# The result of a GNN and expert layer leaves in indirect scatters from GpSimd instead of plain stores from SP

## The reference

```python
def reference(x, adj, ...):
    # _L0_gnn_ref
    h = jnp.einsum('bnd,ed->bne', x, fc_in_w) + fc_in_b
    def euler_step(h, _):
        ax = jnp.einsum('nm,bmd->bnd', adj_mx, h)
        f = alph * 0.5 * (ax - h) + h @ w_eff - h + x0
        return (h + dt * f, None)
    h, _ = jax.lax.scan(euler_step, h, None, length=N_STEPS)
    # _moe
    for e in range(E):
        h = jax.nn.gelu(tokens @ w1[e] + b1[e], approximate=False)
        y = h @ w2[e] + b2[e]
        out = out + combine[:, e:e + 1] * y
    ...
    x = x + _L0_gnn_ref(_layernorm(x, axis=-1), adj, ...)
    x = x + _L0_ffn_ref(_layernorm(x, axis=-1), ...)
    return x
```

## Time and profile before

| | us |
|---|---|
| median of 2 runs | 624.26 (621.85 to 626.67) |
| span of the profiled execution | 619.0 |
| PE busy | 566.9 |
| DVE busy | 473.5 |
| ACT busy | 290.9 |
| POOL busy | 250.2 |
| DMA queue q1 (all DMAs that SP issues), share of 16 engines | 20.9% |

### The profile page before, as it was taken

One profiled execution on the slowest core, in us unless ns is written; L12 is line 12 of the kernel. 1 busy time (PEld: TensorE's weight loads), 2 busy tenths in 40 slices (PEclk: granted clock), 3 DMA queues, 4 the chain that ended last, 5 costly groups with the idle time before them and its releaser, 6 DMA issues.

```text
span 619.0 us, 9553 instructions
## 1 busy us (share of the span) xinstructions
PE 566.9 (92%) x3023; PEld 481.9 (78%) x3023; DVE 473.5 (76%) x1090; ACT 290.9 (47%) x477; POOL 250.2 (40%) x155
## 2 busy tenths in 40 slices
PE   3999999998999799998999799998999799998796
PEld 2778988976898588976898588976898588976574
DVE  5799776779676976779676976779676985579666
ACT  4322131367415662367415662367415672257574
POOL 2230320447213751447313761447313761147355
PEclk9999999999999999999999999999999989998899
DMA  5100010360105200250105300360105200350141
GB/s 181 35 0 1 0 35 1 107 202 1 34 2 210 95 17 17 104 203 0 34 2 197 107 17 17 104 203 0 34 2 191 80 17 19 104 171 0 43 164 35
DMA packets 25759, 43.15 MB, mean 70 GB/s; under 512 B 1462, under 2 KB 20236, under 8 KB 23820
## 3 DMA queue, kind: packets, MB, share of 16 engines
q1 hardware_dynamic: 25740, 42.91, 20.9%
HBM read 38.45 MB, written 4.46 MB: 69 GB/s over the span
## 4 chain that ended last, share of the span: by engine, by line
PE 63%; DVE 20%; issue 9%; ACT 3%; POOL 2%; DMA 1%; DVEq 0%; POOLq 0%; SPq 0%; ACTq 0%
PE bank L954 19%; PE bank L956 18%; PE bank L955 18%; DVE work L818 6%; DVE scr L579 3%; DVE bn L561 2%; PE bank L1080 2%; DVE scs L557 2%; POOL scs L348 2%; DVE x L579 2%; ACT work L494 2%; DVE mv L567 1%; PE bank L973 1%; PE bank L1094 1%; DMA work<-in_adj_dram 1%
## 5 line engine op out<-in xcount | busy, mean ns | idle before, releaser
L348 POOL TENSOR_TENSOR scs<-work,scs 128x512 fp32r<-128x512 f32 x96 | 153.1, 1617 | 103.5 <-ACT scs L397 103.3
L397 ACT ACTIVATE scs<-work 128x512 fp32r<-128x512 f32 (+1 forms) x129 | 82.8, 642 | 53.6 <-DVE work L818 52.3
L494 ACT ACTIVATE work<-bank,cols 128x512 f32<-128x512 f32 x128 | 86.8, 679 | 27.3 <-PE bank L956 27.0
L818 DVE TENSOR_TENSOR work<-work,GT 128x512 f32<-128x512 f32 x90 | 87.9, 990 | 9.6 <-ACT work L494 8.9
L337 POOL TENSOR_TENSOR rstd<-ve,nhalf 128x8 f32<-128x8 f32 x16 | 29.7, 1856 | 113.6 <-DVE ve L575 113.6
L954 PE MATMUL bank<-M,GT 128*128 128x384 f32 x192 | 65.6, 342 | 0.1
L955 PE MATMUL bank<-M,GT 128*128 128x384 f32 x192 | 65.0, 339 | 0.0
L956 PE MATMUL bank<-M,GT 128*128 128x384 f32 x192 | 65.0, 338 | 0.0
L557 DVE TENSOR_TENSOR GT<-bank,GT 128x512 fp32r<-128x512 f32 x48 | 32.2, 687 | 38.3 <-ACT GT L397 38.3
L954 PE MATMUL bank<-scs,w2s 128*128 128x512 f32 x128 | 56.3, 440 | 4.4 <-DVE scs L557 2.7
L397 ACT ACTIVATE GT<-bank 128x512 fp32r<-128x512 f32 x48 | 27.7, 594 | 67.5 <-PE bank L956 63.3
(11 more groups left out here) (188 smaller groups left out, 1382.1 us busy)
## 6 DMA issues: line engine op xcount, KB each, us to landing
GT<-comb_rows SPq DMA_DIRECT2D x8, 1536.0 KB, 6.8
Q<-comb_rows SPq DMA_DIRECT2D x16, 512.0 KB, 5.8
GT<-comb_rows SPq DMA_DIRECT2D x7, 1024.0 KB, 6.2
xn<-in_x_dram SPq DMA_DIRECT2D x16, 256.0 KB, 7.6
out_dram<-outs SPq DMA_DIRECT2D x16, 256.0 KB, 2.2
GT<-comb_rows SPq DMA_DIRECT2D x7, 512.0 KB, 4.3
work<-in_adj_dram SPq DMA_DIRECT2D x4, 256.0 KB, 5.4
Q<-in_L_ffn_w_dram SPq DMA_DIRECT2D x2, 512.0 KB, 5.9
```

Of the source, the lines that this page charges most:

```text
L348: nc.gpsimd.tensor_tensor(scs[:, i % RING, 1, :], scaled[:, i % 3, :], scs[:, i % RING, 0, :].bitcast(FP32), ALU.subtract).then_inc(sc_lo_ ...
L397: return nc.scalar.activation(dst, src, ACT.Copy)
L494: nc.scalar.activation(hid[:, i % 2, :], bank[UP_BANK[i % 3]][:, :], ACT.Gelu, bias=cols[:, B1_COL + e:B1_COL + e + 1]).then_inc(gelu_done, 1)
L818: v.tensor_tensor(scaled[:, i % 3, :], hid[:, i % 2, :], bank[REP_BANK[i % 2]][:, :] if by_pe else rep(i), ALU.mult).then_inc(sc_ready, 1)
```

## The change

The two plain stores per group leave SP. In their place POOL issues, for each batch, four indirect scatters; each takes 128 partitions of `outs[:, b, t, :]` and writes them to 128 rows of the output, whose row numbers stand in a column of an integer tile `out_row`. POOL makes `out_row` once with an iota and adds 1024 (`GB * N`) to all of it for each group in `next_rows`, after it has waited for all scatters issued before. `add_out` on DVE now waits for `row_ready`, which `next_rows` counts up, instead of `out_stored`. On POOL `store(g - 1)` stands at the end of iteration g, `next_rows(g - 1)` after the first `inverse_root`, and iteration 1 is written out ahead of the loop. SP only waits at its end for all scatters (16 x 8 x 8 = 1024).

```diff
--- before.py
+++ after.py
@@ -86,6 +86,8 @@
         rank_i = sb("rank_i", [P, T, E], I32)
         rank = sb("rank", [P, T, E])
         nhalf = sb("nhalf", [P, T])
+        out_row = sb("out_row", [P, GB, NT], I32)
+        out_step = sb("out_step", [P, GB, NT], I32)
 
 
         xn = sb("xn", [P, NT, GB, D])
@@ -192,6 +194,7 @@
 
         out_add = sem("out_add")
         out_stored = sem("out_stored")
+        row_ready, store_go = sem("row_ready"), sem("store_go")
         LN_OWN = T + 2
         RT_OWN = 23
 
@@ -244,7 +247,6 @@
         @block.sync
         def _(sp):
             sp.sem_inc(out_add, 1)
-            sp.sem_inc(out_stored, 1)
             sp.dma_start(alpha_rows[:, :], alpha.rearrange("(t p) -> t p", p=P)).then_inc(alpha_in, 16)
 
             def load_x(g):
@@ -255,11 +257,6 @@
                 sp.wait_ge(x0_ready, g)
                 sp.wait_ge(xg_copied, g)
                 load_x(g)
-
-            def store(h):
-                for b in range(GB):
-                    sp.wait_ge(out_add, 1 + GB * h + b + 1)
-                    sp.dma_start(of_group(out_v, h, b), outs[:, b, :, :]).then_inc(out_stored, 16)
 
             load_x(0)
             for t in range(NT):
@@ -311,13 +308,10 @@
             with sp.Fori(1, GROUPS - 2) as g:
                 expert_weights(g - 1, g)
                 next_x(g + 2)
-                store(g - 1)
             for g in range(GROUPS - 2, GROUPS):
                 expert_weights(g - 1, g)
-                store(g - 1)
             expert_weights(GROUPS - 1)
-            store(GROUPS - 1)
-            sp.wait_ge(out_stored, 1 + 32 * GROUPS)
+            sp.wait_ge(out_stored, 16 * T * GROUPS)
 
 
         @block.gpsimd
@@ -329,7 +323,9 @@
             nc.gpsimd.iota(rank_i[:, :, :], pattern=[[0, T], [-1, E]], base=E, channel_multiplier=0)
             nc.gpsimd.memset(b2_raw, 0.0).then_inc(b2_zero, 1)
             nc.gpsimd.memset(nhalf[:, :], -0.5).then_inc(pool_own, 1)
-            pool.wait_ge(pool_own, 2)
+            nc.gpsimd.iota(out_row[:, :, :], pattern=[[N, GB], [P, NT]], base=-GB * N, channel_multiplier=1)
+            nc.gpsimd.memset(out_step[:, :, :], GB * N).then_inc(pool_own, 1)
+            pool.wait_ge(pool_own, 3)
             nc.gpsimd.tensor_copy(rank[:, :, :], rank_i[:, :, :]).then_inc(pool_const, 1)
 
             def inverse_root(n, g):
@@ -347,6 +343,26 @@
                 pool.wait_ge(sc_hi, ITEMS * h + i + 1)
                 nc.gpsimd.tensor_tensor(scs[:, i % RING, 1, :], scaled[:, i % 3, :],
                                         scs[:, i % RING, 0, :].bitcast(FP32), ALU.subtract).then_inc(sc_lo_pool, 1)
+
+            def store(h):
+
+                for b in range(GB):
+                    pool.wait_ge(out_add, 1 + GB * h + b + 1)
+                    if b == 0:
+                        pool.wait_ge(row_ready, h + 1)
+                    pool.sem_inc(store_go, 1)
+                    for t in range(NT):
+                        nc.gpsimd.indirect_dma_start(
+                            out=out.rearrange("b n c -> (b n) c"),
+                            out_offset=bass.IndirectOffsetOnAxis(ap=out_row[:, b, t:t + 1], axis=0),
+                            in_=outs[:, b, t, :], in_offset=None).then_inc(out_stored, 16)
+
+            def next_rows(h):
+
+                if not (isinstance(h, int) and h == 0):
+                    pool.wait_ge(out_stored, 16 * T * h)
+                nc.gpsimd.tensor_tensor(out_row[:, :, :], out_row[:, :, :], out_step[:, :, :],
+                                        ALU.add).then_inc(row_ready, 1)
 
             def residual(h):
 
@@ -367,6 +383,8 @@
                     residual(g - 1)
                 if not final:
                     inverse_root(0, g + 1)
+                if not first:
+                    next_rows(g - 1)
                 pool.wait_ge(xg_copied, g + 1)
                 pool.wait_ge(q_ready, T * g + T)
                 nc.gpsimd.tensor_tensor(Q[:, 0], Q[:, 0], xg[:, :, :, :], ALU.add).then_inc(xq_ready, 1)
@@ -380,15 +398,19 @@
                             item_low(g - 1, i)
                         if i == 2:
                             inverse_root(1, g)
+                    store(g - 1)
 
             iteration(0, first=True)
-            with pool.Fori(1, GROUPS - 1) as g:
+            iteration(1)
+            with pool.Fori(2, GROUPS - 1) as g:
                 iteration(g)
             iteration(GROUPS - 1, final=True)
             residual(GROUPS - 1)
             for i in range(ITEMS):
                 if i not in LOW_DVE:
                     item_low(GROUPS - 1, i)
+            next_rows(GROUPS - 1)
+            store(GROUPS - 1)
 
 
         @block.scalar
@@ -802,7 +824,7 @@
             def add_out(h, b):
                 dve.wait_ge(ot_mm, GB * h + b + 1)
                 dve.wait_ge(res_ready, h + 1)
-                dve.wait_ge(out_stored, 1 + 32 * h)
+                dve.wait_ge(row_ready, h + 1)
                 v.tensor_tensor(outs[:, b, :, :], bank[OT_BANK[b]][:, :].rearrange("p (t c) -> p t c", c=D),
                                 res[:, :, b, :], ALU.add).then_inc(out_add, 1)
```

## The result

The changed kernel took 640.24 us (median of 2 runs, 640.18 to 640.30) against 624.26 us (2 runs, 621.85 to 626.67): ratio 1.0286, interval 1.0226 to 1.0346. Run again later, six executions against 18 of the kernel before, it took 634.79 us (633.03 to 643.51) against 622.9 us: ratio 1.0176, interval 1.0134 to 1.0218. So the change costs about 1.8% in the larger set of runs, whose interval reaches over the 2%, and nearly 3% in the first pair. Each series of runs can hold a single run that is over 1.5% above the fastest of its kernel at a lower granted clock, as 643.51 and 632.85 here; the medians and ranges hold such runs, the ratios and intervals leave them out.

A forecast was written before the change was run, and what follows sets the result against it. The chain that ended last was put on PE for 63% and DVE for 20%. Loop 0, last group's experts 0 and end 6.95 gave 7.0 us, added to 624.26 for 631.2 us; range 625.5 to 646.

The forecast's parts named there:

- the case: Whole kernel: time within 2% of the kernel before, counted as no change; chance 0.69.
- c: Time for which one scatter holds POOL, chosen as 1.2 us between bounds of 0.39 and 2.41 us.
- rivals 1 and 3: First: scatter over 1.6 us, loop pays, 658.6 us, chance 0.22. Second: cheap addresses, under 0.65, 624.3 us, chance 0.08.
- The loop costs nothing: Six loop turns: four scatters fit between the adds, residual ends 1.2 us before DVE wants it; cost 0.
- Rival 2: Loop: DVE's work holds up POOL's address writing, 1.9 us per scatter there, 1.2 at the end; 646.7 us, chance 0.08.
- Last group's experts: 0 at c = 1.2, bound 1.22: Start of last group's experts: residual and item 0 end at 592.58, just in time; beyond 1.22, each 0.1 costs up to 0.4.
- DVE's scaling of item 3 (592.67) waits for that `item_low`: Last group's experts: this scaling reuses the buffer of item 0's `item_low`, so POOL's work must end by 592.67.
- The end: 8c - 2.65 = 6.95: Program end: nothing covers the last eight scatters, run from 613.8 with 2.55 us behind them; cost 6.95 us.
- the last needs 2.2 us to land and 0.35 us remain as before: Program end: after the last scatter, landing and the unchanged remainder take 2.55 us until the span ends.
- Median 5.3 us over the profiled span: Whole run: the median of the runs shown, 624.26 us, is 5.3 us above the profiled span of 619.0.
- the cases for "slower by over 2%": Whole kernel: nearly all of rival 1's 0.22, the lock-out and a little of rival 4; chance 0.30 together.
- rival 4: Order no longer fits for another reason, such as a first scatter costing several us once; 625 to 645 us, chance 0.07.

The follow-up runs named there:

- The four extra scatters: Changed kernel plus four more scatters to an unread tensor behind the second add of groups 0 to 6 (92 in the run): 673.59 us, ratio 1.0821.
- 16 plain: Changed kernel with one plain DMA from POOL in place of each four scatters: 624.95 us, ratio 1.0038.
- 22: Changed kernel with only the first of each batch's four scatters in groups 0 to 6, all eight in the last: 632.67 us, ratio 1.0175.
- the kernel with 56: Changed kernel with the last group stored by SP as before, the loop's scatters left in: 623.34 us, ratio 1.0016.
- With 8: Kernel before with only the last group's two stores replaced by eight scatters from POOL: 625.34 us, ratio 1.0038.

## Why the prediction was right, and where it was not

The forecast was 631.2 us, 1.1% slower, most likely within 2%, with a range of 625.5 to 646. The repetition, 1.8% slower, agrees with the case as far as its interval (1.3 to 2.2%) can tell; the first measurement, 2.9% slower, lies in the range but on the other side of the 2%. The cost was 11.9 us by the medians of the repetition and 16.0 by the first, where 7.0 were forecast. The range held both partly by luck: it was made wide for c, which was nearly exact, and was used up by two other things, the DRAIN and, in the first measurement, the clock. Step by step:

- **c = 1.2 us.** Measured 1.26 (0.96 and 0.30). The choice between rows came out well, though the rows did not compel it. It also puts away rivals 1 and 3, whose conditions were c over 1.6 and under 0.65.
- **The loop costs nothing.** Right in mechanism: no wait of DVE; 1.0016 without the last group's scatters. The margin was smaller than reckoned: the residual was to end 1.2 us before DVE's first Q add and ends 0.5 us before it (241.96, predicted 241.7, but this group's adds come 0.5 us earlier than before). The pause of 0.8 us ahead of the first scatter, which the sum left out, makes the difference. The four extra scatters show that the room was real and small.
- **Rival 2, the lock-out.** It did not occur: 56 of the 64 scatters take 0.95 or 0.96 us, beside DVE's work in the loop and without it at the end, and the eight longer ones (0.98 to 1.18) are the first of each group. The rule of the Trainium skill, page "SBUF — State Buffer", section "Who interferes with whom", is not tested by these rows: it names copy, cast and tensor_scalar for the two-port mode, and beside the scatters DVE ran operations on two tensors, reductions, reciprocals and statistics, and of those three only one tensor_scalar, over 8 columns.
- **Last group's experts: 0 at c = 1.2, bound 1.22.** Wrong; measured +1.7 us. The step "DVE's scaling of item 3 (592.67) waits for that `item_low`" took the wrong row. The scalings start at 586.40, 587.25, 589.39, 591.32 and 592.67, and counted from item 0 the fourth, 591.32, is item 3. So the residual and the `item_low` had 1.35 us less than reckoned. On top, the first scatter starts 0.8 us behind the end of the add (590.52 to 591.33), for which the sum had 0.15. In the changed kernel the residual starts at 596.10, the `item_low` behind it at 598.43, and item 3's scaling, due at 591.32 + 6.53 = 597.85, waits for it:

```profile
599.87 0.69 DVE L840 TENSOR_TENSOR work<-work,bank 128x512 f32<-128x512 f32 x1 [3.09 <-POOL scs L344]
```

  2.0 us late, of which 1.7 are left at the first output add. With the right row and the pause, the four scatters are on the path from c = (591.32 - 584.8 - 2.35 - 1.28) / 4 = 0.72, not from 1.22.
- **The end: 8c - 2.65 = 6.95.** Measured 11.0, so by the prediction's own sign ("if the end grows by other than 8c - 2.65") this step was wrong. The scatters themselves were right, 9.8 us for eight where 9.6 were reckoned. The pause of 0.8 us ahead of the first is missing again. And 5.5 us follow the last scatter where 2.55 were reckoned: the step "the last needs 2.2 us to land and 0.35 us remain as before" took the landing for the last thing that ends. The landing was indeed seen by 634.1. What ended last was POOL's closing DRAIN, which the trace of before showed only for a POOL that had issued no DMA: there it ended at 612.7, 0.1 us behind POOL's last work. Together 0.8 + 0.2 + 3.0 = 4.0, the difference.
- **Median 5.3 us over the profiled span.** Wrong as a step. A run lies some 2.1 us above the span of its own execution (640.3 and 638.2). By that the profiled execution of before, 619.0, would be a run of 621.1, near the faster of the two shown (621.85), and 624.26 is the mean of that one and a slower one. To which run that trace belongs is not on record. The sum is unharmed, since it is a difference, but spans of single executions differ by several us through the clock alone.
- **The chances.** Of the cases for "slower by over 2%", none occurred, unless the DRAIN is counted under rival 4, "another reason", which named no such mechanism; what brought the first measurement over the line was, by its profiled execution, 4 us more at the end, 1.7 at the last experts and 7 from the clock. None of the three was in the sum, and the last is, by the medians of the repetition, not a cost of the change.

**The DRAIN.** How long it goes on after POOL's last instruction, and how long SP then stands still (its wait at line 61), in the kernels with such a DRAIN:

| DMAs that POOL issued | 0 | 8 | 16 plain | 22 | 56 | 64 | 92 |
|---|---|---|---|---|---|---|---|
| DRAIN ends after POOL's last work, us | 0.1 | 1.66 | 2.68 | 2.27 | 4.67 | 5.3 | 7.6 |
| SP stands still, us | 0.2 | 0.3 | 0.7 | 1.0 | 0.2 | 4.0 | 6.3 |

In the kernel with 56, whose last transfers SP issued, it starts earlier and is hidden: POOL's last work ends at 617.75, the DRAIN at 622.4, SP at 623.4. With 8 it ends at 622.9, together with the last landing that SP saw (622.8), so there it adds next to nothing. From 22 scatters to 64, with the same end of the program, it grows by 3.0 us, or 0.07 us for each scatter of groups 0 to 6, long landed ones included; from 64 to 92 by 0.08. It goes neither by bytes (the 16 plain DMAs move the same 4 MB as the 64 scatters) nor by the count of DMAs alone (the 16 plain ones have more than the 22 scatters). Why it goes on is open. So the kernel pays for the loop's scatters at the end of the program: 5.3 us behind the last scatter with all 64 and 1.66 with the last eight alone, 3.6 of the 11.0 us.

## What to carry to other kernels

Cost a transfer on POOL by its DMA instructions and not by bytes: an indirect scatter of 128 rows (64 KB) took 1.26 us of POOL from start to start, a plain DMA of 512 rows (256 KB) 0.75 us, and the first after a wait for DVE started 0.6 to 1.0 us behind DVE's end. Inside a loop either is free as long as it fits in the room ahead of what POOL does next; at the end of the program all of it is on the path. Count what closes the program too, and look for the engine that ends last there, since a wait put down to a queue that was idle hides it. And before a difference of 1% between two single executions is explained by a mechanism, compare the granted clock of each turn and ask for more runs.

## What was not expected of the hardware

- POOL's closing DRAIN grows with the scatters that POOL issued over the whole run, from 1.66 us behind its last work at 8 to 7.6 us at 92.
- The granted clock falls to half for 3.4 or 6.8 us at a time, in different turns in different executions of one kernel, and filling most of PE's idle time ahead of the transposes of z did not stop it.
- 32 unused bytes in each partition made the kernel before 0.9% faster, with all matmuls the same and a turn of 68.9 in place of 69.35 us; a shift of 96 bytes gave the shorter turn too, one of 64 did not.
- A semaphore from PE reached DVE some 2.8 us after the matmuls of its tile stand finished in the trace, whose matmul ends are modelled, in the one kernel in which scatters ran beside it.
